# Offset convolution of a deformable block on 32x64 array tiles, two chunks at a time in three phases

## The reference, cut to what matters

```python
x = x + _L0_conv_ref(_gn(x), ...)       # 3x3 depthwise, then three 32x32 channel mixes (one 3x3 conv, "conv1")
x = x + _L1_conv_ref(_gn(x), ...)       # deformable part, then a 3x3 conv ("conv2") with bias

def _deform(x, w_off):                  # x: (8, 32, 128, 128), w_off: (64, 32, 3, 3)
    off = _conv(x, w_off, 1)            # two offsets for every element
    off = off.reshape(B * C, H * W, 2)
    coords = off + grid
    rows = clip(coords[..., 0]); cols = clip(coords[..., 1])
    r0, r1, c0, c1 = floor(rows), ceil(rows), floor(cols), ceil(cols)
    # four gathers, bilinear mix
```

## Time and profile before

| | |
|---|---|
| three runs | 723.59, 724.89, 725.79 us |
| median | 724.89 us |
| the profiled execution | span 724.3 us from first to last instruction, 0.6 us below the median of the runs; no other time is given for it |
| PE busy | 684.9 us (95%) |
| DVE busy | 525.0 us (72%) |
| POOL busy | 478.0 us (66%) |
| ACT busy | 465.9 us (64%) |
| DMA | 115.64 MB, mean 160 GB/s |

### The profile page before, as it was taken

The page is one execution under the profiler, slowest core; times in us unless marked ns, Lnnn a source line. Parts: engine busy times, 40 slices in busy tenths (PEclk is TensorE's granted clock), DMA queues, the critical chain, the costliest instruction groups (busy, mean ns, idle before and its releaser), DMA issues.

```text
span 724.3 us, 10746 instructions
## 1 busy us (share of the span) xinstructions
PE 684.9 (95%) x3500; PEld 244.5 (34%) x3500; DVE 525.0 (72%) x1037; ACT 465.9 (64%) x809; POOL 478.0 (66%) x413
## 2 busy tenths in 40 slices
PE   4799979999999699999999999999999999999986
PEld 4333333333333233333333333333333333333322
DVE  3587988779935858657985598657984775578892
ACT  7487777676728824766567666577656775577860
POOL 4004867888594844868758666886658668787760
PEclk9999999999999989999999999999999999999999
DMA  8958927889459895699948997599957626477555
GB/s 140 186 109 149 136 60 164 174 178 205 121 129 247 163 199 131 157 223 173 201 108 194 200 219 163 132 231 179 207 132 173 158 60 143 116 163 179 123 126 135
DMA packets 140189, 115.64 MB, mean 160 GB/s; under 512 B 15168, under 2 KB 114016, under 8 KB 140128
## 3 DMA queue, kind: packets, MB, share of 16 engines
q1 hardware_dynamic: 116096, 103.12, 68.2%
q10 hardware_dynamic: 24032, 11.78, 9.0%
HBM read 31.59 MB, written 16.78 MB: 67 GB/s over the span
## 4 chain that ended last, share of the span: by engine, by line
PE 61%; SPq 11%; DVE 4%; ACT 3%; POOL 3%; issue 2%; DMA 2%; DVEq 0%; POOLq 0%; ACTq 0%
PE off_ps L781 30%; PE c_ps L670 26%; SPq L388 3%; SPq L469 3%; PE c_ps L681 2%; PE c_ps L685 2%; SPq L451 2%; DMA mapb<-mapa 1%; SPq L420 1%; DVE other_row L1422 1%; ACT other_row L975 1%; ACT off_abs L988 1%; POOL row_diff L1199 1%; SPq L461 1%; PE c_ps L689 1%
## 5 line engine op out<-in xcount | busy, mean ns | idle before, releaser
L1422 DVE COPY_PREDICATED other_row<-down_ps,row_diff 128x768 f32<-128x768 int32 x128 | 124.7, 1027 | 114.8 <-ACT down_ps L986 114.8
L781 PE MATMUL off_ps<-x1a,wo 128*64 128x512 f32 x768 | 176.8, 594 | 0.8 <-DVE other_row L1434 0.8
L781 PE MATMUL off_ps<-x1b,wo 128*64 128x512 f32 x768 | 176.1, 592 | 0.0
L670 PE MATMUL c_ps<-xb,w 128*64 128x512 f32 x336 | 149.8, 593 | 4.2 <-DVE xb L1495 2.0
L670 PE MATMUL c_ps<-mapb,w 128*64 128x512 f32 x336 | 150.8, 594 | 1.6 <-DVE x1a L1407 1.6
L672 PE MATMUL c_ps<-xa,w 128*64 128x512 f32 x336 | 149.8, 593 | 0.0
L975 ACT ACTIVATE other_row<-row_diff 128x768 f32<-128x768 f32 x128 | 100.8, 835 | 67.4 <-POOL row_diff L1201 46.5
L1216 POOL TENSOR_TENSOR other_row<-other_row,x_strips 128x512 f32<-128x512 f32 x48 | 57.2, 1192 | 128.1 <-DVE other_row L1434 128.1
L672 PE MATMUL c_ps<-mapa,w 128*64 128x512 f32 x294 | 131.7, 594 | 0.0
L986 ACT ACTIVATE down_ps<-off_ps,bias_o 128x512 f32<-128x512 f32 x64 | 41.9, 655 | 108.0 <-PE off_ps L781 100.5
L1217 POOL TENSOR_TENSOR other_col<-other_col,other_row 128x512 f32<-128x512 f32 x64 | 86.3, 1349 | 31.4 <-DVE other_row L1434 31.3
(11 more groups left out here) (135 smaller groups left out, 990.3 us busy)
## 6 DMA issues: line engine op xcount, KB each, us to landing
mapa<-mapped SPq DMA_DIRECT2D x224, 65.0 KB, 2.0
x1b<-x1a SPq DMA_DIRECT2D x28, 520.0 KB, 6.5
mapb<-mapa SPq DMA_DIRECT2D x28, 520.0 KB, 8.3
out_dram<-x1a SPq DMA_DIRECT2D x49, 256.0 KB, 4.7
xb<-in_x_dram SPq DMA_DIRECT2D x48, 256.0 KB, 9.0
xa<-in_x_dram ACTq DMA_DIRECT2D x40, 256.0 KB, 7.3
x_strips<-x1a SPq DMA_DIRECT2D x112, 81.2 KB, 2.1
x_strips<-x1a SPq DMA_DIRECT2D x112, 65.0 KB, 2.1
```

Of the source, the lines that this page charges most:

```text
L670: nc.tensor.matmul(bank[0:64, :], weights[:, kx, :], rows_b[:, of, kx:kx + W], start=(kx == 0), stop=(kx == 2))
L781: last = nc.tensor.matmul(off_ps[k % 2][64 * t:64 * t + 64, CH * n:CH * n + CH], wo[wpar][:, kx, side:side + 2 * C], rows[:, b:b + 7:2, kx ...
L1422: last = dve.copy_predicated(other_row[n][:, :, KR // 2 * odd:KR // 2 * odd + KR // 2, :], bass.AP(tensor=rows.tensor, offset=rows.offset ...
```

## The change

Each tap (ky, kx) of the offsets' convolution becomes a matmul of its own on a tile of 32 array rows (one row block q of `x1a`) by 64 columns. Four row blocks by two column halves make eight tiles in the array. The weights `wo` are laid out for nine taps. A pair of chunks (left and right halves together, "u") is computed at once in the four banks of both `off_ps`, in three phases (ky), and behind each phase stand the jobs of `pair_jobs`. `x1b`, its copies and its writes are gone. The eighth bank: two mask banks `mask_ps` (row, column), and `c_ps` has two banks instead of three. VectorE multiplies both halves in one instruction by the lengths in SBUF. Chunks are ordered so that k and k+1 are the left and right half of the same rows. ScalarE, VectorE and SyncE orders are rewritten around pairs, and the last image's copies are shared out otherwise.

```diff
+        def pair_jobs(i, u):
+            behind, n = [[], [], []], 0
+            for job in jobs_behind(i, 2 * u) + jobs_behind(i, 2 * u + 1):
+                behind[n].append(job)
+                if job[0] in ("x1", "c2"):
+                    n = min(n + 1, 2)
+            return behind
...
-        down_ps = pb("down_ps", [P, CH])
-        c_ps = [pb(f"c_ps{n}", [P, 4 * W]) for n in range(3)]
+        mask_ps = [pb(f"{name}_mask_ps", [P, CH]) for name in ("row", "col")]
+        c_ps = [pb(f"c_ps{n}", [P, 4 * W]) for n in range(2)]
...  SyncE
-                    sp.wait_ge(off_done, NK * i)
-                    copy_x1b(i % 3, 1)
...
-                    sp.wait_ge(off_done, NK * i + 4)
-                    copy_x1b((i + 1) % 3, 0)
...  TensorE
+            def offsets_phase(wpar, par, u, ky):
+                for kx in range(3):
+                    for r in range(4):
+                        q = slice(Q * ((r + ky) % 4), Q * ((r + ky) % 4) + Q)
+                        for t in range(2):
+                            b = 2 * NJ * t + NJ * (u // 2) + u % 2 + (r + ky) // 4
+                            last = nc.tensor.matmul(off_ps[r % 2][64 * t:64 * t + 64, CH * (r // 2):CH * (r // 2) + CH],
+                                                    wo[wpar][q, 3 * ky + kx, :],
+                                                    x1a[par][q, b:b + 7:2, kx:kx + W],
+                                                    start=(ky == 0 and kx == 0), stop=(ky == 2 and kx == 2))
+                last.then_inc(off_phases, 1)
...
+                for u in range(NP):
+                    if NP * i + u >= 1:
+                        pe.wait_ge(col_mask_ready, NK * i + 2 * u)
+                    for ky, jobs in enumerate(pair_jobs(i, u)):
+                        if NP * i + u >= 1 or ky >= 1:
+                            pe.wait_ge(off_phases, PHASES * (NP * i + u) + ky)
+                        offsets_phase(i % 2, i % 3, u, ky)
+                        for job in jobs:
+                            job_of(job)
...  ScalarE, one pair (e, o = 2u, 2u + 1)
+                    copy_rows(i, e)
+                    for job in behind[0] + behind[1]:
+                        evacuate(job)
...
+                    act.wait_ge(off_phases, PHASES * (NP * i + u + 1))
+                    row_mask(i, e)
+                    lengths(i, e)
+                    col_mask(i, e)
+                    lengths(i, o)
+                    for job in behind[2][:1]:
+                        evacuate(job)
+                    row_mask(i, o)
+                    col_mask(i, o)
+                    copy_rows(i, o)
...
+                    if nxt and u and ("x1", i + 1, 7) in sum(pair_jobs(i, u - 1), []):
+                        pad_x1(i + 1, (i + 1) % 3)
...
+                    if nxt and u == NP - 1:
+                        clamp(i + 1, 0)
+                    for job in behind[2][1:]:
+                        evacuate(job)
+                    sum_far(i, e)
+                    sum_far(i, o)
...  VectorE, one pair
+                    for job in behind[0] + behind[1]:
+                        follow(job)
+                    deform(i, e)
+                    for job in behind[2]:
+                        follow(job)
...
+                    if after and u == (2 if i else 1):
+                        x_stats(i + 2, 0)
+                    deform(i, o)
+                    if nxt and ("x1", i + 1, 7) in sum(behind, []):
+                        x1_norm(i + 1, (i + 1) % 2, (i + 1) % 3)
+                    if after and u == (2 if i else 1):
+                        x_stats(i + 2, 1)
                         x_norm(i + 2, i % 2)
...  VectorE, deform
-                step(dve.scalar_tensor_tensor(own, down, bias_o[i % 2][:, :], own, ALU.add, ALU.mult))
...
-                dve.scalar_tensor_tensor(beside, down, bias_o[i % 2][:, :], beside, ALU.add, ALU.mult).then_inc(off_used, 1)
+                dve.tensor_tensor(beside_and_own, beside_and_own,
+                                  bass.AP(tensor=lengths.tensor, offset=lengths.offset,
+                                          ap=[list(lengths.ap[0]), [0, 2], [2, CH]]),
+                                  ALU.mult).then_inc(products_ready, 1)
```

More of the change, by code:

```diff
@@ L452, in load_xb @@
                       .then_inc(loaded[half], DMA)
[L454 to L460, removed]
-                sp.dma_start(to_lower[:, :, of], lower[:, :, of]).then_inc(x1b_copied[half], DMA)
-                sp.dma_start(to_upper[:, :, of], upper[:, :, of]).then_inc(x1b_copied[half], DMA)
             def move_rows(tile, first, n, moved):
@@ L610, in _ @@
                     wait_apart(x1_pads, v + 1)
-                    for half in range(2):
-                        copy_x1b(0, half)
                     wait_apart(conv2_done, 8 * v)
@@ L1060, in _ @@
                         pad_mapped(i, i % 3, 0)
[L1061 to L1063 removed]
+                        clamp(i, 1)
+                    if u == 2:
                         pad_mapped(i, i % 3, 1)
[L1065 to L1069 removed]
@@ L1077, in _ @@
+                    if not nxt and u == 1:
+                        pad_end(i % 3)
+                    if after and i and u == NP - 1:
+                        pad_x(i + 2, i % 2)
+                    if nxt and u == NP - 1:
[4 more added lines that the diff above has]
+                    sum_far(i, o)
                     for half in range(2):
-                        if prev and i + 2 < NB and 4 * half + 3 in groups:
+                        if prev and after and 4 * half + 3 in groups:
@@ L1113, in _ @@
             with act.If(any_far != 0):
+                act.sem_inc(off_used, NK * NB)
                 with act.Fori(0, NB) as b:
@@ L1203, in row_steps @@
                                    ALU.subtract).then_inc(diff_ready, 1)
-            row_steps(0, 0)
+            for side in range(2):
+                row_steps(0, 0, side)
             for i in range(NB):
@@ L1479, in _ @@
-                    if prev:
-                        for m in (LAST_CONV2 if nxt else END_CONV2)[k]:
-                            add_group(i - 1, (i - 1) % 2, (i - 1) % 3, m, bank("c2", i - 1, m))
-                    if after and k == (4 if i else 1):
+                    for job in behind[0] + behind[1]:
[3 more added lines that the diff above has]
+                        follow(job)
+                    if not nxt and u == END_BIAS // 2:
+                        prepare_conv2(i, i % 2, i % 3)
```

345 lines of the change are left out of this document (142 added, 203 removed).

## The result

| | before | after |
|---|---|---|
| median, us | 725.2 (4 runs, 723.6 to 725.8) | 813.15 (4 runs, 811.8 to 813.7) |
| ratio | | 1.120 (95% interval 1.115 to 1.124) |
| span of the profiled execution, us | 724.3 | 810.0 |
| matmuls in flight, us (share) | 684.9 (95%) | 665.5 (82%) |

What follows compares the result with a forecast made beforehand. TensorE bounds the kernel before; afterwards a loop through SyncE holds steady images at 85.0 us. Start 27, steady images 6 and end 5 add 38 to 724.3, with 0.6 for the median 763 us; own range 740 to 785, full range 695 to 800.

Steps and rivals of the forecast that it cites:

- The phase: Offsets' convolution on TensorE: six slots of 0.43 us, 2.57 us a phase, plus 0.1 us per tile-shape switch (bounds 0 and 0.3).
- The rival of tiles not side by side: Offsets' convolution: tiles don't run fully side by side, phases take 3.24 us, 820 us in all; chance 0.15.
- The masks' chain behind a pair: ScalarE's masks and lengths behind a last phase: TensorE idles 4.8 us where no groups stand behind, as in image 0.
- image 1 begins at 145.8: End of image 0: exposed masks, slow clock and x_norm, less the phases' gain, start image 1 22.5 us later than before.
- +6.5: Image 1: strips not yet moved at its start and a late first row mask raise the delay from 22.5 to 29 us.
- pads end at S+47.7: Steady image, ScalarE's side: from the store's landing S through evacuations, masks and two pairs to the pads' end, 47.7 us.
- SyncE 36.3: Steady image, SyncE's queue: strips 20.3, mapa 10.1, store 3.3 to 5 and landing 2.5, together 36.3 us.
- with the durations of before 88: Steady image: the loop through SyncE takes 88 us at the earlier durations, against 85.0 forecast.
- only the start is lost: Steady images: if SyncE's loop has slack, VectorE's norms bound them at 81 us, 746 us in all; chance 0.1.
- TensorE as the bound: Whole kernel: ScalarE and VectorE come by in time, six images keep what the phases save, 690 us; chance 0.24.
- +5: Image 7 and the end: two deforms and GpSimd behind the last phase instead of one, less moved copies, 5 us more.
- 3 later than before: Image 7: pairs with 0, 2, 2 and 1 groups end their last phase at 61 us, 3 us later than before.

Runs made afterwards that it cites:

- a_xnorm: Changed kernel with image 2's statistics and norm behind image 0's first pair instead of its second: 801.6 us, ratio 1.106 to the kernel before.
- a_behind: Changed kernel with all groups of a pair behind its third phase in images 0 and 7: 791.3 us, ratio 1.088 to the kernel before.
- a_pads: Changed kernel with ScalarE writing x1's pads before it waits for the pair's last phase: 773.8 us, ratio 1.068 to the kernel before.
- a_all: Changed kernel with early pads, early image 2 norm, groups behind third phases in images 0 and 7, two more groups inside image 7's pairs: 747.75 us, ratio 1.029.
- a_all_one_tap: a_all with one column tap of three in the offsets' convolution, two thirds of its matmuls left out: 730.55 us, ratio 1.007 to the kernel before.
- a_fill: Changed kernel with unread matmuls in idle stretches behind pairs of images 0 and 7 and ahead of image 2's first sum: 806.8 us, ratio 1.115.
- a_end: a_behind with two more of image 6's conv2 groups placed inside image 7's pairs: 792.3 us, ratio 1.089 to the kernel before.

## Why the prediction was wrong

**The phase: right.** 2.77 us with a switch, eight tiles side by side; a switch 0.18 instead of 0.1, inside the bounds. The rival of tiles not side by side fell; that its 820 us is near the result is chance. The Trainium skill's 3.07 times for four row tiles (TensorE: Matmul & The Clock Gate, Measured speedup vs the span model) isn't what this stream of eight tiles shows: an estimate from that figure makes a slot 0.56 us, and it is 0.43. The Trainium skill also says that a change of tiling mode drains the engine (TensorEngine Tiling (Array Packing), Tiling Modes); 0.18 us for a switch fits that.

**The masks' chain behind a pair: right in mechanism and size.** Forecast 4.8 us; ScalarE's masks behind image 0's first pair released TensorE after 4.79:

```profile
74.17 4.99 PE L775 MATMUL off_ps<-x1a,wo 32*64 32x512 f32 x48 [4.79 <-ACT col_mask_ps L978]
```

The same row gives the clock's price: the phase behind the gap takes 4.99 us instead of 2.84, 2.15 more where I had 1.9.

**Image 0, "image 1 begins at 145.8": 9 us short.** It began at 154.7. Image 2's norm came 8.7 us late for its sum instead of 7, and TensorE waited 2.85 us for the offsets' scaled weights (L1376), which the forecast did not have; the pads' 7.6 it had (8). The other 4 us I have not split; the slow clock behind two gaps more than forecast is part of it. a_xnorm gives 12 us back, and a_behind lets image 1 begin 19 us earlier, so norm and bare masks are where image 0's loss is.

**Image 1, "+6.5": +15.3.** The strips that start late were in the forecast. What was not: TensorE's idle 4.5 us at a later hand-over (200.3) and the slow clock behind it and behind the pads. Images 1 and 2 together gave 8.6 where I had 4.5. This part I have from the trace alone; no run tests it.

**Steady images, "pads end at S+47.7" and "SyncE 36.3": the loop was right, both terms too small, and the error counts four times.** S is the landing of the store. In image 4 of after:

```profile
403.80 20.66 SPq L402 DMA_DIRECT2D x_strips<-x1a  x32
424.57 10.58 SPq L473 DMA_DIRECT2D mapa<-mapped  x16
438.94 1.20 SPq L439 DMA_DIRECT2D out_dram<-x1a  x1
442.34 0.36 ACT L923 ACTIVATE x1a<-c_ps,bias 32x128 f32<-32x128 f32 x1 [6.62 <-issue]
491.61 0.93 ACT L857 ACTIVATE x1a<-dve_columns 128x66 f32<-128x66 f32 x3
492.56 21.26 SPq L402 DMA_DIRECT2D x_strips<-x1a  x32
```

Strips to evacuation 38.5 us where I had 36.3, evacuation to the end of the pads 50.2 where I had 48.7; 88.7, which is the period. The mean of four images is 88.9 against the forecast's 85.0: 16 us of the miss. On SyncE's side the term that was too small is the store. I took 3.3 us for its issues; the earlier trace rows have 5.0 (381.68 to 386.68), and here it takes 4.95. On the other side the last phase ends at S+42.5 and not S+38.7. The two groups behind the late evacuation ran at half clock, which the forecast has behind the gaps of image 0 but not here:

```profile
443.30:447.44 4.14, 4.12 (x12) 1.25 (x13) 4.14 (x6) 3.67 (x5) 0.00 (x0) 0.53 0.98 213
```

In this window five slots take 0.85 us each instead of 0.43, at a granted clock of 0.53.

ScalarE stood 6.6 us for the store (3.25 before; this view names no releaser, but the instruction's line waits for the store) with TensorE idle for 5.25 us until 443.3, as the prediction's test had it. The pads end 68.5 us into the image. The kernel before has 51.3. The forecast's own terms give 16 + 47.7 = 64, while its signs name 59, so the two don't agree. Nor does its "with the durations of before 88" follow from the earlier trace rows: 39.75 us from strips to the store's last issue, 2.5 to land and 48.7 make 91, and with that its own range would have ended some 12 us higher, near 797. I had seen that the pads were 8 us later and taken it for a fixed cost; a_pads shows it was the whole of the loop's loss, and moving one call gives it back. That `x_norm`, two banks and switches bound a steady image at 81 ("only the start is lost") came close to what is left then (82.8 in a_all), but for another reason, as far as the traces show: GpSimd's fourth chunk.

**TensorE as the bound, 690 us with a chance of 0.24: wrong, and the chance was too high.** With half the matmuls (a_all_one_tap) and the pads early a steady image still takes 81 us. The row of 95% busy TensorE said who was last, not how near the next was: the ring through SyncE and three engines needed 81 of 83.4 us already, if it is the same in the kernel before, which these runs don't show.

**Image 7 and the end, "+5": +23.5, the worst step.** I had priced every hand-over there at 4.8 us and the slow clock behind it at nothing, although image 0's sum has it. The first hand-over takes 9.99 us, and all three phases behind a gap run slow. ScalarE first, then TensorE:

```profile
700.29 1.58 ACT L952 ACTIVATE other_row<-row_diff 128x768 f32<-128x768 f32 x2 [5.14 <-POOL row_diff L1193]
706.67 1.11 ACT L962 ACTIVATE off_abs<-off_ps,bias_o 128x1024 f32<-128x1024 f32 x1 [2.14 <-POOL mapped L1222]
708.97 5.02 PE L775 MATMUL off_ps<-x1a,wo 32*64 32x512 f32 x48 [9.99 <-ACT col_mask_ps L978]
729.84 4.83 PE L775 MATMUL off_ps<-x1a,wo 32*64 32x512 f32 x48 [4.74 <-ACT col_mask_ps L978]
750.40 4.53 PE L775 MATMUL off_ps<-x1a,wo 32*64 32x512 f32 x48 [4.74 <-ACT col_mask_ps L978]
```

Two chunks reach GpSimd in one lot now, and the row differences of image 7 stand behind both. In every image ScalarE waits there; only image 7 has no group to lay over it. So the last phase ended 73.2 us into the image where I had 61: 5.2 us by the first hand-over, 5.9 by the slow phases (a_fill, with its clock up, has 4.2 of it back). My "3 later than before" was also misread, as the kernel before ends its last offsets 56.1 us into the image:

```profile
681.36 2.75 PE L781 MATMUL off_ps<-x1b,wo 128*64 128x512 f32 x12
```

The stretch up to this point thus grew by 17.1 of the 23.5 us, and the stretch from there to the end by 6.4 (46.6 instead of 40.2). In it GpSimd's last sum ends 18.3 us behind the last offsets' matmul, where it was 14.6: 3.7 us for two chunks in one lot. The additions behind both deforms, my first explanation of the rest, fell with a_end. The other 2.7 us stay open.

## What to carry to other kernels

When the bound engine's accumulators lose their second set, price the whole release chain at every hand-over, with the slow clock behind it, and look for those with nothing to lay over them (first and last stage): here laying groups over them gave 22 us back. Once an engine's work shrinks, follow the ring that closes over images (a store, the buffer it frees, the next load behind it in a queue); one write on it came late, each steady image paid 6 us for it, and moving one call gave that back. Moving a transfer ahead in a full queue only changed who waits, and cost 9 us.

## What the runs showed of the hardware

A masked copy of 128 x 512 with its mask in PSUM takes 0.73 us, with the mask in SBUF 1.10 (data from another tile) to 1.18 (data within one tile), means of 64. With the mask in SBUF the mean of GpSimd's 32 row differences of 330 elements went from 0.97 to 1.19; the median stayed at 0.89 to 0.90, so more of them than before took about twice the usual time (1.88 at most). That VectorE's copies beside them are the reason is not tested. A switch between 128-row tiles and 32-row tiles costs 0.18 us (the mean of both ways) in a stream of 0.43 us slots. Behind a gap of 4.8 us a phase takes 4.99 us instead of 2.84, at a granted clock of 0.55; filling such gaps by unread matmuls gave some 6 us of 813, not told from none, as the gap itself remains.
